# Fourth node buffer, 71 slots of dense products and high parts on VectorE in a two-hop graph kernel

## What is computed

```python
h = jnp.maximum(_layernorm(x), 0.0)
x = x + relu(segment_sum(where(edge_type == 0, h[src] @ W_data.T + b_data,
                               h[src] @ W_control.T + b_control), dst) + h @ W_self.T + b_self)
h = jnp.maximum(_layernorm(x), 0.0)
norm = deg_inv_sqrt[row] * deg_inv_sqrt[col]
y, total = h, h
for _ in range(2):                       # the two hops
    y = segment_sum(y[row] * norm[:, None], col)
    total = total + y
out = x + total / 3
```

## Time and profile before

| | us |
|---|---|
| median of three runs | 3672.07 (3669.55 to 3674.48) |
| the profiled execution | 3670.85 |
| its span, first to last instruction | 3668.83 |
| hop 1, from TensorE's first lead step to its last dense step | 1951.67 to 2808.10 |
| hop 2, the same | 2825.13 to 3651.60 |

### The profile page before, as it was taken

The page is one execution under the profiler, slowest core; times in us unless marked ns, Lnnn a source line. Parts: engine busy times, 40 slices in busy tenths (PEclk is TensorE's granted clock), DMA queues, the critical chain, the costliest instruction groups (busy, mean ns, idle before and its releaser), DMA issues.

```text
span 3668.8 us, 64228 instructions
## 1 busy us (share of the span) xinstructions
PE 3144.8 (86%) x23900; PEld 2855.9 (78%) x23900; DVE 1793.7 (49%) x4171; ACT 2652.7 (72%) x2875; POOL 2472.8 (67%) x2610
## 2 busy tenths in 40 slices
PE   5578788888888867667667999999997999999998
PEld 3368677777677755445457999999997999999998
DVE  6864655554545578888883232333333222222223
ACT  3366666776667654554546889999995899999997
POOL 2477667777777777777774666666664766666666
PEclk8889899998899976776768999999998999999999
DMA  8623333333333375555556788888889878887876
GB/s 241 177 84 91 97 94 102 113 87 112 100 85 112 105 230 183 184 187 183 189 182 208 228 242 247 240 251 241 253 252 317 245 230 233 235 235 233 235 233 199
DMA packets 444207, 687.74 MB, mean 187 GB/s; under 512 B 62390, under 2 KB 373569, under 8 KB 435699
## 3 DMA queue, kind: packets, MB, share of 16 engines
q1 hardware_dynamic: 343827, 441.27, 37.6%
q0 software_dynamic: 99200, 241.92, 23.8%
q10 hardware_dynamic: 864, 0.39, 0.1%
HBM read 511.64 MB, written 171.70 MB: 186 GB/s over the span
## 4 chain that ended last, share of the span: by engine, by line
PE 45%; DVE 3%; ACT 1%; issue 1%; DMA 1%; POOL 0%; DVEq 0%; SPq 0%; POOLq 0%; ACTq 0%
PE wide L1491 39%; PE sums_bank L1367 3%; PE sums_bank L1365 1%; ACT strip_ring L1283 1%; PE wide L1403 1%; DVE flat L1900 1%; DVE flat L1897 1%; DMA stage<-strips 1%; POOL rows L1114 0%; DVE xin L1754 0%; DMA hop_table<-stage 0%; DVE scaled L1756 0%; DVE scaled L1746 0%; ACT scaled L1194 0%; DVE stage L1898 0%
## 5 line engine op out<-in xcount | busy, mean ns | idle before, releaser
L1114 POOL DMA_INDIRECT flat<-typed_table,index x1333 | 1297.8, 974 | 464.6 <-issue 400.6
L1283 ACT CAST strip_ring<-stage 128x1792 fp32r<-128x1792 uint8 x896 | 1495.0, 1687 | 144.9 <-PE wide L1491 126.3
L1491 PE MATMUL wide<-table_parts,strip_ring 128*128 128x256 f32 x12544 | 1542.6, 285 | 38.7 <-ACT strip_ring L1283 31.5
L1491 PEld LDWEIGHTS wide<-table_parts,strip_ring 128*128 128x128 f32 x12544 | 1528.0, 194 | 42.6 <-issue 25.7
L1114 POOL DMA_INDIRECT rows<-hop_table,index x1162 | 1111.6, 957 | 608.5 <-issue 314.4
L1265 ACT CAST stage<-wide 128x392 uint16<-128x392 f32 x1344 | 547.2, 517 | 464.6 <-PE wide L1403 463.6
L1403 PE MATMUL wide<-stage,flat 128*128 128x196 bf16 x2688 | 445.8, 286 | 301.1 <-DVE flat L1900 164.3
L1403 PEld LDWEIGHTS wide<-stage,flat 128*128 128x128 bf16 x2688 | 211.7, 108 | 517.6 <-DVE flat L1900 202.4
L1417 PE MATMUL turned_bank<-typed_ring,table_parts 128*128 128x256 f32 x3920 | 538.3, 298 | 76.8 <-ACT typed_ring L1276 70.4
L1845 DVE SCALAR_TENSOR_TENSOR sums<-sums_bank,in_upper,sums 128x128 f32 (+1 forms) x459 | 160.4, 350 | 876.8 <-PE sums_bank L1367 674.5
L1417 PEld LDWEIGHTS turned_bank<-typed_ring,table_parts 128*128 128x128 f32 x3920 | 509.2, 203 | 96.5 <-issue 59.4
(11 more groups left out here) (183 smaller groups left out, 1400.3 us busy)
## 6 DMA issues: line engine op xcount, KB each, us to landing
stage<-strips SPq DMA_DIRECT2D x896, 224.0 KB, 3.7
strips<-stage SPq DMA_DIRECT2D x64, 1568.0 KB
table_parts<-hop_table SPq DMA_DIRECT2D x28, 896.0 KB, 9.7
flat<-typed_table,index POOLq DMA_INDIRECT x1333
rows<-hop_table,index POOLq DMA_INDIRECT x1162
resid<-xin SPq DMA_DIRECT2D x50, 256.0 KB, 3.7
xin<-resid SPq DMA_DIRECT2D x50, 256.0 KB, 4.9
typed_table<-flat SPq DMA_DIRECT2D x49, 256.0 KB, 2.4
```

Source lines behind the costliest of these rows:

```text
L1114: pool.indirect_dma_start(out=gathered(k, o % RING, c), out_offset=None, in_=tables[k], in_offset=bass.IndirectOffsetOnAxis(ap=index[:, ch ...
L1283: act.copy(strip_ring[:, number % STRIP_RING], counts_ring[place]).then_inc(strip_cast, 1)
L1491: last = pe.matmul(wide[:, nth % 4, 0:PARTS * P], strip_ring[:, number % STRIP_RING, b - first, :], table_parts[:, b, :, :].rearrange("p n ...
```

## The change

Six things are changed:

1. The hops have a fourth buffer of `xin` (HOP_XIN). It lies in columns 0 to 511 of `index`, whose groups are used in pass 0 alone.
2. The dense steps are dealt over 71 of the 73 slots of a hop instead of 69. By the planner most slots hold six steps, and slots 66 to 70 of hop 1 hold six each.
3. In hop 1 the high part is made by VectorE, in `finish`, between L1756 and L1760. ScalarE's `finish` is called in pass 0 alone.
4. The lead is dealt over the extra slots as 3, 1, 2, 4, 4, 4 instead of 3 in each. This moves casts on ScalarE around its `finish` of the last batch of pass 0; TensorE's order of steps is the same.
5. A reload between the hops may start one slot after the last use of its piece, not in the slot of it. With the steps dealt anew, the reloads stand at slots 67, 67, 68, 68, 69, 69, 69, 70, 71, 71, 71, 75, 75 and 77 of hop 1.
6. A semaphore that nobody waits for (`typed_degree`) is dropped.

The last four events of hop 1 and of hop 2 become batch 14 at slot 66, 23 at 69, 15 at 70 and 24 at 72.

```diff
-DENSE_SLOTS = 69
+SLOTS_BEHIND_DENSE = 2
-LEAD_AT_ONCE = 3
+LEAD_AT = (3, 1, 2, 4, 4, 4)
+HOP_XIN = 4
+    dense_slots = hop_groups - SLOTS_BEHIND_DENSE
...
         rest = steps_per_hop - lead_steps[k]
-        return lead_steps[k] + min(rest, -(-(i + 1) * rest // DENSE_SLOTS))
+        return lead_steps[k] + min(rest, -(-(i + 1) * rest // dense_slots))
...
-    events += [spread_out(hop_wanted(k), XIN) for k in range(1, HOPS + 1)]
+    events += [spread_out(hop_wanted(k), HOP_XIN) for k in range(1, HOPS + 1)]
...
-        xin_place = [n % FIRST_XIN if n < total else n % XIN for n in range(events_all)]
+        xin_place = [n % FIRST_XIN if n < total else n % HOP_XIN for n in range(events_all)]
+
+        def xin_of(n, general):
+            if xin_place[n] < XIN:
+                return xin[:, xin_place[n], :]
+            if general:
+                return flat[:, row_words - BATCH:row_words]
+            return index[:, 0:BATCH].bitcast(F32)
...
             if i >= slots_of(k) and k < HOPS:
-                first = (i - slots_of(k)) * LEAD_AT_ONCE
-                return [step_number(k + 1, j) for j in range(first, min(first + LEAD_AT_ONCE, lead_steps[k + 1]))]
+                first = sum(LEAD_AT[:i - slots_of(k)])
+                return [step_number(k + 1, j) for j in range(first, min(first + LEAD_AT[i - slots_of(k)], lead_steps[k + 1]))]
...
             if k:
-                return slot_of_step(1, last_step_with(piece))
+                return slot_of_step(1, last_step_with(piece)) + 1
...
@@ scalar engine, finish
                     normalise(scaled_of(n, k), xin[:, xin_place[n], :], batch_rstd[:, 0, :], batch_shift, held(s)).then_inc(fresh_ready, 1)
-                if k < HOPS:
                     act.wait_ge(scaled_ready, n + 1)
                     act.copy(high_of(n, k, s, general), in_blocks(scaled_of(n, k)[:, 0:held(s) * P], held(s))
                              ).then_inc(high_ready, 1)
...
-                        if finishing and k < HOPS:
+                        if finishing and k == 0:
                             finish(finishing[0], k, finishing[1], False)
...
@@ vector engine, finish
-                nodes_in = xin[:, xin_place[n], 0:columns]
+                nodes_in = xin_of(n, general)[:, 0:columns]
...
                 dve.wait_ge(scaled_ready, n + 1)
+                if k:
+                    dve.tensor_copy(high_of(n, k, s, general), in_blocks(values, blocks)).then_inc(high_ready, 1)
                 dve.wait_ge(high_ready, n + 1)
```

More of the change, by code:

```diff
@@ L580, in gnn_kernel @@
         tile_read = semaphore("tile_read")
-        xin_in = semaphores("xin_in", XIN)
+        xin_in = semaphores("xin_in", HOP_XIN)
         own_rows_in = semaphores("own_rows_in", 2)
         degree_read = semaphore("degree_read")
-        typed_degree = semaphore("typed_degree")
         fresh_made = semaphore("fresh_made")
@@ L596, in gnn_kernel @@
         table_stored = semaphores("table_stored", 2)
-        resid_stored = semaphores("resid_stored", XIN)
+        resid_stored = semaphores("resid_stored", HOP_XIN)
         out_stored = semaphores("out_stored", 2)
@@ L623, in scaled_of @@
             return scaled[:, 0 if k == 0 else n % 2, :]
-        xin_place = [n % FIRST_XIN if n < total else n % XIN for n in range(events_all)]
+        xin_place = [n % FIRST_XIN if n < total else n % HOP_XIN for n in range(events_all)]
[5 more added lines that the diff above has]
+            return index[:, 0:BATCH].bitcast(F32)
+        assert BATCH <= first_group * CHUNKS
         def xin_uses(n):
@@ L802, in reloads_of_slot @@
             return [piece for slot, piece in reload_orders[k] if slot == i]
-        assert all(lead_steps[k] <= LEAD_AT_ONCE * LAST for k in range(1, HOPS + 1))
+        assert len(LEAD_AT) == LAST and all(lead_steps[k] <= sum(LEAD_AT) for k in range(1, HOPS + 1))
         def edge_round(i):
@@ L895, in _, with load_nodes @@
                          pair_tile.rearrange("p (k e) n -> p k (e n)", k=PAIR_TILES)).then_inc(pairs_stored, 16)
-            def load_nodes(n, k, s, before):
+            def load_nodes(n, k, s, before, general):
                 place = xin_place[n]
@@ L913, in load_nodes @@
                     sp.wait_ge(resid_stored[xin_place[before]], 16 * xin_uses(before))
-                    sp.dma_start(in_blocks(xin[:, place, :]), of_batch(resid, s)).then_inc(xin_in[place], 16)
+                    sp.dma_start(in_blocks(xin_of(n, general)), of_batch(resid, s)).then_inc(xin_in[place], 16)
             def load_own(s, place, landed):
@@ L923, in store_nodes @@
                     sp.wait_ge(resid_ready, n + 1)
-                    sp.dma_start(of_batch(resid, s), in_blocks(xin[:, xin_place[n], :])).then_inc(resid_stored[xin_place[n]], 16)
+                    sp.dma_start(of_batch(resid, s), in_blocks(xin_of(n, general))).then_inc(resid_stored[xin_place[n]], 16)
                     sp.wait_ge(low_ready, n + 1)
@@ L955, in _ @@
                     for s in range(total):
-                        load_nodes(k * total + s, k, s, (k - 1) * total + s)
+                        load_nodes(k * total + s, k, s, (k - 1) * total + s, True)
                         if k == 0:
@@ L1016, in load_event @@
                 def load_event(k, n, s):
-                    load_nodes(n, k, s, event_of[k - 1][s] if k else None)
+                    load_nodes(n, k, s, event_of[k - 1][s] if k else None, False)
                     if k == 0 and s >= TYPED_BATCHES:
@@ L1252, in _ @@
                         act.copy(ring_index[:, :], index[:, ds(g * CHUNKS, CHUNKS)]).then_inc(rest_index, 1)
-                    for s in range(total):
-                        finish(k * total + s, k, s, True)
+                    if k == 0:
+                        for s in range(total):
+                            finish(s, k, s, True)
                 act.nop()
@@ L1696, in take_degrees @@
                 dve.tensor_scalar(linked_now, degree, 0.0, None, ALU.is_gt)
-                dve.tensor_scalar(spread_now[:, 1, :], degree, 1.0, None, ALU.max).then_inc(degree_read if s >= TYPED_BATCHES else typed_degree, 1)
+                read = dve.tensor_scalar(spread_now[:, 1, :], degree, 1.0, None, ALU.max)
+                if s >= TYPED_BATCHES:
+                    read.then_inc(degree_read, 1)
             def finish(n, k, s, source, read, general):
```

## The result

The changed kernel takes 3647.5 us (median of 4 runs, 3646.32 to 3649.07), the kernel before on the same chip 3670.81: a ratio of 0.9937 (95% interval 0.9925 to 0.9949), 0.6% or 23 us less. The profiled execution has a span of 3647.3 us against 3668.83, 21.5 less. The forecast was 34.5 less.

The account below looks back on a forecast made before the run. TensorE, at 0.1196 us per matmul, was taken as the bound, everything over that pace as loss; gains of 12.5 + 4.3 + 9.1 + 4.7 + 3.9 = 34.5 us off 3670.85 give 3636 us, range 3629 to 3652.

Parts of the forecast that it names:

- High parts on VectorE: Slots 1 to 65 of hop 1: without ScalarE's copy and wait they fall to 740.4 us, gain 12.5.
- That a copy costs GpSimd nothing: Hop 1: a gather's issue overlapping a VectorE copy took 0.97 us against a mean of 0.96.
- The lead: Start of hop 1: ScalarE reaches the last batch's square root after four casts, not six; gain 4.3 us (2.5 to 5).
- The end of hop 2: Behind the last dense step: less work left with 71 slots, 11.4 us for 17.2; gain 3.9 (2.5 to 4.5).
- Reloads a slot later, and the fourth buffer: Last dense slots of hop 1: less waiting in SyncE's queue, loss 2 us for 11.1; gain 9.1 (3 to 11).
- 71 slots between the hops: From the first sum behind the dense steps to hop 2: seventh lead step sooner, gain 4.7 us (0 to 7).
- T + 26: Between the hops: seventh lead step starts 26 us after the first sum behind the dense steps, for 32.6 before.
- The blocker that the term named: Between the hops: ScalarE makes batch 24's high part only at 2834.66, after six casts, ahead of the counts' loads.
- the crowd moves along: Rival, chance 0.12: around hop 1's end counts land late, lead steps wait for reloads; 9.1 and 4.7 gone, 3650 us.
- a sign of being wrong: Wrong if hop 1 slots stretch where VectorE copies, GpSimd no longer waits for TensorE, or lead steps wait for reloads.

Follow-up runs that it names:

- Eight copies: The changed kernel with VectorE's copy of the high part made eight times instead of once per batch of hop 1: 3647.12 us.
- the second profile of the same kernel: The changed kernel run once more as it is, beside two further orders: median 3644.35 us, 0.9925 of before; profiled run 3646.28 us.
- Thin reloads: The changed kernel with each reload between the hops moving one of its seven blocks, waits and order kept: 3629.29 us.
- High parts alone: The kernel before with one part of the change, high parts of hop 1 made by VectorE: 3659.89 us.
- the best kernel: The changed kernel with six loads of counts ahead of late reloads, the last three reloads behind the last rows and three more counts: 3632.36 us, 0.989 of before.

## Why the prediction was right and wrong

The sign and the range held (3647.5 in 3629 to 3652); the forecast of 3636 was 11 too low. One term came out below its own lower bound (-5.5 for 0 to 7); the range held because the others came near or above the middles of theirs. By its steps:

- *High parts on VectorE, 12.5*: right, 740.64 for slots 1 to 65 with this part alone and 753.50 for slots 1 to 68 in the whole, all of it TensorE busy. The copy, taken as 0.45 us, measured 0.429, and VectorE's slack hid it. That a copy costs GpSimd nothing was read from one gather, a lucky pick: beside the same pair of a clearing and a copy one at 2411.69 took 1.42 us. Eight copies show that it does not matter here.
- *The lead, 4.3*: right; 4.4 in the stage, and 4.3 when the line is put back.
- *The end of hop 2, 3.9*: right; 4.1 in the stage and when the slots are put back.
- *Reloads a slot later, and the fourth buffer, 9.1*: the mechanism was right for the reloads and the size was off: 6.7. The fourth buffer had no part in it (26.0 us for the two slots with three). Slots 69 and 70 still lose 4.4, for 2, with DMA at a share of 1.06 and 349 GB/s: the loss by bytes was 2.7, and I had let the buffered counts swallow some of it; nothing shows that they did.
- *71 slots between the hops, +4.7*: this step failed; it was -5.5. The term put the seventh lead step at T + 26 and it came at T + 32.55: 6.5 of the 10.2 us by which it missed. The other 3.7 lie behind that step, where it took the time of before over; 2.5 of them are the slow clock of slot 0, which the second profile of the same kernel does not have (there the term would be -3.3). What was wrong ahead of the step? First, the store of batch 15 was given 4.0 us to land, from the earlier trace rows, where the last reload had been issued 11 us earlier and DMA was at a share of 0.78 in the next four us (2820 to 2824 of before); here the last of three reloads was 5 us earlier, DMA at 1.12 (2800 to 2804), and it took some 7, and batch 23's took 7.9, for which VectorE's batch 24 waited (low parts at T + 20.6, not T + 15). So the loads of the counts were issued at T + 24.0, not T + 19, and took 8.6 us to the first matmul, for 4.7 before. Thin reloads, which give T + 14.3 for the low parts and T + 24.0 for the seventh step, show that the bytes are the cause. Second, the bill for moving the reloads a slot later was written only into the dense slots. Three of them then fall behind T: the reloads of before have the seventh step 3 us sooner, and slot 1 of hop 2 3.5 to 5.7.

The blocker that the term named, ScalarE's copy of batch 24 at 2834.66, was the last link before, but little hung on it alone. High parts alone took it away, and the seventh lead step went only from T + 32.6 to T + 31.0. Close behind it stood the landings, one step back in SyncE's queue.

The result is nearer to the rival "the crowd moves along" (3650) than to the forecast. It held in its sum: of the 9.1 and 4.7 together 1.2 was left. It held in part in its form: a lead step waited for reloads 10 to 12, as it said, which the prediction had also named as a sign of being wrong; but the dense slots kept most of their gain. I gave it 0.12, on the ground that SyncE's waits were gone and fewer rows were fetched. The reloads' bytes were still there, three of them now behind T.

Open: what sets the clock of slot 0 in a given run (below); what the fourth buffer is worth, of which there is one run alone; and how much of the 12.25 us that thin reloads leave is the order in SyncE's queue, which no run changes together with the bytes.

## What to carry to other kernels

A transfer put off to a later place keeps its bytes: write its price into the new place too, and ask there which small store or load stands behind it on the same queue and who waits for that to land. Take a landing time only from a row with as much in front of it. Where several waits stand in one queue, order the small transfers that start a chain (counts, rows) ahead of the large ones whose reader comes later, and stop where the reader's own loads become late.

## What the runs showed of the hardware

DMA traffic stood near 350 GB/s in the last dense slots of three kernels: 347 to 353 at a share of 1.05 to 1.06. That this is a ceiling was not tested. Stores of 512 KB issued some 5 us or less behind three reloads took 7 to 8 us until what waited for their landing went on, for 4.0 in the earlier trace rows. The time in which SyncE issues three reloads differs too, and not by their bytes alone: 5.80 us in the changed kernel and 2.45 with a seventh of the bytes, but 1.69 at full size in the best kernel (2812.44 above).

An idle time of about 3 us ahead of slot 0's dense steps sometimes brought a slow clock and sometimes none. In the changed kernel 3.01 us of idle were followed by 12.85 us for 84 matmuls, at a mean granted clock of 0.77, so partly at 1.2 and partly at 2.4 GHz. In another run of the same kernel 3.33 us were followed by 10.31 at 1.00:

```profile
2842.89:2855.58 12.69, 12.69 (x84) 12.69 (x85) 1.27 (x3) 8.13 (x5) 9.46 (x10) 0.77 0.67 205
```

```profile
2841.77:2851.92 10.15, 10.15 (x85) 10.15 (x85) 1.27 (x3) 8.14 (x5) 7.57 (x8) 1.00 0.75 225
```

With the reloads of before it was 3.27 us of idle and 10.30, with 69 slots 3.29 and 12.71. So these 2.5 us are not set by the length of the idle time alone, and a difference of that size between two single profiles says nothing of an edit.
